# A fused patch, attention and expert kernel: patches resident in the first stage, rows loaded and normed in groups beside the patch products

## What is computed

```python
p = x.reshape(B, C, NH, PH, NW, PW).transpose(0, 2, 4, 3, 5, 1).reshape(B, NH * NW, PH * PW * C)
h = jnp.einsum('bnd,hd->bnh', p, Wp) + b + pos           # 16 images x 64 patches x 256
h = jnp.concatenate([h, txt], axis=1)                    # 16 x 141 x 256
h = h + L0_attn(layernorm(h), Wq, Wkv, Wo)               # 8 heads, l2-normed q and k
h = h + L0_ffn(layernorm(h), ...)                        # 8 experts, top 2
h = h + L1_attn(layernorm(h), ...)
h = h + L1_ffn(layernorm(h), ...)
```

## Time and profile before

| | |
|---|---|
| time, median of 3 runs | 1245.07 us (1244.85 to 1264.2) |
| time of the profiled execution | 1249.64 us |
| its span, first to last instruction | 1247.8 us |
| PE busy | 1066.6 us (85%) |
| DVE busy | 677.3 us (54%) |
| ACT busy | 417.8 us (33%) |
| POOL busy | 367.7 us (29%) |
| mean granted TensorE clock | 0.912 of 2.4 GHz |

### The profile page before, as it was taken

The page is one execution under the profiler, slowest core; times in us unless marked ns, Lnnn a source line. Parts: engine busy times, 40 slices in busy tenths (PEclk is TensorE's granted clock), DMA queues, the critical chain, the costliest instruction groups (busy, mean ns, idle before and its releaser), DMA issues.

```text
span 1247.8 us, 22340 instructions
## 1 busy us (share of the span) xinstructions
PE 1066.6 (85%) x7200; PEld 881.0 (71%) x7200; DVE 677.3 (54%) x1577; ACT 417.8 (33%) x868; POOL 367.7 (29%) x238
## 2 busy tenths in 40 slices
PE   5489979887199999999999994978999999875765
PEld 4368867776178888888888882546878888764634
DVE  0366636666734444444444445975566766545555
ACT  0245555663022222222222212444344444343313
POOL 0000000222461460661506005507444544312104
PEclk8799989998599999999999997998798999786977
DMA  6411144331264414323300003520100011020243
GB/s 240 141 43 47 45 151 138 103 102 35 93 179 153 144 40 144 103 85 140 131 26 31 27 17 110 165 86 26 26 25 25 26 29 28 11 81 14 72 153 123
DMA packets 68699, 104.84 MB, mean 84 GB/s; under 512 B 15141, under 2 KB 53637, under 8 KB 66285
## 3 DMA queue, kind: packets, MB, share of 16 engines
q1 hardware_dynamic: 44941, 52.13, 13.8%
q0 software_dynamic: 5904, 34.61, 7.8%
q10 hardware_dynamic: 17776, 17.04, 4.0%
HBM read 74.60 MB, written 30.41 MB: 84 GB/s over the span
## 4 chain that ended last, share of the span: by engine, by line
PE 66%; DVE 15%; issue 8%; DMA 5%; ACT 4%; POOL 1%; SPq 0%; DVEq 0%; ACTq 0%; POOLq 0%
PE psum L1717 19%; PE psum L1732 10%; PE psum L1573 6%; PE psum L1853 5%; PE psum L1830 4%; PE psum L1725 3%; PE psum L1637 2%; DMA work<-in_patches 2%; PE psum L1843 1%; PE psum L1540 1%; PE psum L1928 1%; PE psum L1877 1%; PE psum L1855 1%; PE psum L1876 1%; PE psum L1976 1%
## 5 line engine op out<-in xcount | busy, mean ns | idle before, releaser
L1221 DVE TENSOR_TENSOR work<-work,psum 128x512 f32<-128x512 f32 x86 | 59.1, 687 | 218.8 <-ACT work L719 218.8
L1717 PE MATMUL psum<-w_high,xT_high 128*128 x344 | 139.5, 406 | 1.1 <-DVE xT_low L1215 1.1
L1717 PE MATMUL psum<-w_low,xT_high 128*128 x344 | 135.2, 393 | 0.0
L1717 PE MATMUL psum<-w_high,xT_low 128*128 x344 | 134.8, 392 | 0.0
L719 ACT ACTIVATE work<-psum 128x512 f32<-128x512 f32 x86 | 51.4, 598 | 207.2 <-PE psum L1717 207.2
L1732 PE MATMUL psum<-w_high,hidT_high 128*128 x344 | 103.6, 301 | 0.6 <-DVE hidT_low L1228 0.6
L1732 PE MATMUL psum<-w_high,hidT_low 128*128 x344 | 96.1, 279 | 0.0
L1732 PE MATMUL psum<-w_low,hidT_high 128*128 x344 | 96.0, 279 | 0.0
L518 POOL TENSOR_TENSOR w_low<-big,w_high 128x6144 fp32r<-128x6144 f32 x7 | 94.2, 13457 | 0.6
L516 POOL CAST w_high<-big 128x6144 fp32r<-128x6144 f32 x7 | 37.3, 5322 | 188.2 <-PE psum L1732 177.3
L1830 PE MATMUL psum<-wexp,work 128*128 128x282 f32 x256 | 83.4, 454 | 7.9 <-POOL wexp L543 7.7
(11 more groups left out here) (287 smaller groups left out, 2341.8 us busy)
## 6 DMA issues: line engine op xcount, KB each, us to landing
big<-in_w_gu POOLq DMA_DIRECT2D x7, 2048.0 KB, 9.0
work<-v_scratch SPq DMA_DIRECT2D x32, 256.0 KB
big<-in_w_down POOLq DMA_DIRECT2D x7, 1024.0 KB, 11.3
work<-slot_in_scratch SPq DMA_DIRECT2D x43, 128.0 KB, 2.0
slot_out_scratch<-work ACTq DMA_DIRECT2D x43, 128.0 KB, 1.7
v_scratch<-work SPq DMA_DIRECT2D x18, 256.0 KB, 2.0
work<-in_rope SPq DMA_DIRECT2D x18, 192.0 KB, 2.4
work<-in_patches SPq DMA_DIRECT2D x8, 384.0 KB, 4.5
```

The source lines that it names most:

```text
L1221: nc.vector.tensor_tensor(hid[:, s, :], sil[:, s, :], psum[:, 2 * s + 1, :], ALU.mult).then_inc(S("hid_ready"), 1)
L1717: m = nc.tensor.matmul(psum[:, 2 * half + a, :], f32r(x_[:, s, k, :]), f32r(w_[:, ds(at + k * 2 * F + a * F + half * 512, 512)]), start=(k ...
```

## The change

All of it lies in the first stage. Nothing of the computation changes.

- The four pairs of patch tiles get four places (`pt_places`), and SP issues all four loads at the start, each of two tiles, with no wait. The patch weight counts on the first pair's semaphore. Of the row vectors only the first comes at the start; the other four come behind the load of group 0.
- PE's tiles go to four PSUM banks instead of two. Its wait for `w0low` moves behind the first transpose.
- `posb` and `h0s` move from `work` to `wexp`.
- The stores of patch tiles go from ACT to SP. SP loads group 0 of `h` after issuing the stores of tile 3, once the stores of tiles 0 to 2 and the text of six images have landed; group 1 after issuing those of tile 6, once the stores of tiles 0 to 5 have landed; group 2 at the end.
- ACT copies the text in two parts: six images, then, behind the weight of the first attention and once the first part has landed, ten. With no stores to issue, it goes on to `w0high` at once.
- DVE keeps tiles 0 to 4, then norms group 0 and the first two tiles, then keeps tiles 5 to 7, then takes `w0low`.

```diff
-        pt = view(work, 0, 2, PK, P)
-        posb = view(work, 1536, D)
-        h0s = view(work, 1792, 2, D)
+        pt_places = (view(work, 0, 2, PK, P), *(view(work, 4912 + 1536 * n, 2, PK, P) for n in range(3)))
+        posb = view(wexp, 6400, D)
+        h0s = view(wexp, 6656, 2, D)
...
 SP
-            sp.dma_start(wtok_sb, w_tok).then_inc(S("tables_ld"), 16)
-            sp.dma_start(posb, pos_table).then_inc(S("tables_ld"), 16)
-            sp.dma_start(rowv[:, :, :], row_vectors).then_inc(S("tables_ld"), 16)
-            with sp.Fori(0, IMAGES // 4) as i:
+            sp.dma_start(wtok_sb, w_tok).then_inc(S("pt_ld0"), 16)
+            for n in range(IMAGES // 4):
+                sp.dma_start(pt_places[n].rearrange("p o k n -> p o (k n)"), patches[2 * n:2 * n + 2, :, :, :].rearrange("o p k n -> o p (k n)")).then_inc(S(f"pt_ld{n}"), 16)
+                if n == 0:
+                    sp.dma_start(posb, pos_table).then_inc(S("tables_ld"), 16)
+                    sp.dma_start(rowv[:, 0, :], row_vectors[:, 0, :]).then_inc(S("tables_ld"), 16)
+
+            def load_group(g, tiles):
                 for s in range(2):
-                    t = 2 * i + s
-                    sp.wait_ge(S("tok_ps"), t + 1)
-                    sp.dma_start(pt[:, s, :, :], patches[ds(t, 1), :, :, :].rearrange("o p k n -> p (o k) n")).then_inc(S(f"pt_ld{s}"), 16)
-
-            sp.wait_ge(S("h0_st"), 32)
-            for s in range(2):
-                sp.wait_ge(S(f"tok_st{s}"), 32 * (IMAGES // 4 + 1))
-            for g in range(GROUPS):
+                    sp.wait_ge(S(f"tok_st{s}"), 32 * ((tiles + 1 - s) // 2))
                 sp.dma_start(h[:, g * GT:(g + 1) * GT, :], h0_d[g * GT * P:(g + 1) * GT * P, :].rearrange("(t p) d -> p t d", p=P)).then_inc(S(f"h_ld{g}"), 16)
+
+            for t in range(IMAGES // 2):
+                sp.wait_ge(S("tok_ready"), t + 1)
+                for r in range(2):
+                    sp.dma_start(h0_img[2 * t + r, 0:PATCHES, :], h0s[64 * r:64 * r + 64, t % 2, :]).then_inc(S(f"tok_st{t % 2}"), 16)
+                if t == 3:
+                    sp.wait_ge(S("h0_st"), 16)
+                    load_group(0, 3)
+                    sp.dma_start(rowv[:, 1:5, :], row_vectors[:, 1:5, :]).then_inc(S("h_ld0"), 16)
+                if t == 6:
+                    sp.wait_ge(S("h0_st"), 48)
+                    load_group(1, 6)
+            load_group(2, IMAGES // 2)
...
 ACT
-            act.wait_ge(S("pt_ld1"), 16)
-            act.dma_start(h0_img[:, PATCHES:SEQ, :], txt).then_inc(S("h0_st"), 16)
+            act.wait_ge(S("pt_ld0"), 32)
+            act.dma_start(h0_img[0:GT, PATCHES:SEQ, :], txt[0:GT, :, :]).then_inc(S("h0_st"), 16)
+            act.dma_start(const[:, :], constants).then_inc(S("w0_ld"), 16)
+            act.dma_start(wqkv_sb, w_qkv0).then_inc(S("w0_ld"), 16)
+            act.wait_ge(S("h0_st"), 16)
+            act.dma_start(h0_img[GT:IMAGES, PATCHES:SEQ, :], txt[GT:IMAGES, :, :]).then_inc(S("h0_st"), 16)
...
-            with act.Fori(0, IMAGES // 4) as i:
-                for s in range(2):
-                    t = 2 * i + s
-                    act.wait_ge(S("tok_ready"), t + 3)
-                    for r in range(2):
-                        act.dma_start(h0_img[ds(2 * t + r, 1), 0:PATCHES, :].rearrange("o n d -> (o n) d"),
-                                      h0s[64 * r:64 * r + 64, s, :]).then_inc(S(f"tok_st{s}"), 16)
...
 DVE
+            def keep_tok(t):
+                dve.wait_ge(S("tok_ps"), t + 1)
+                if t >= 2:
+                    dve.wait_ge(S(f"tok_st{t % 2}"), 32 * (t // 2))
+                nc.vector.tensor_tensor(h0s[:, t % 2, :], psum[:, t % 4, 0:D], posb, ALU.add).then_inc(S("tok_ready"), 1)
+
+            for t in range(5):
+                keep_tok(t)
 
             def norm_group(g):
-                dve.wait_ge(S(f"h_ld{g}"), 16)
+                dve.wait_ge(S(f"h_ld{g}"), 16 if g else 32)
...
             norm_group(0)
             for t in range(2):
                 normed(xn[:, t, :], t).then_inc(S("xn_ready"), 1)
+            for t in range(5, IMAGES // 2):
+                keep_tok(t)
+            dve.wait_ge(S("act_did"), W0_HIGH)
+            step(nc.vector.tensor_tensor(f32r(w0low), wqkv_sb, w0high, ALU.subtract))
+            dve.sem_inc(S("dve_did"), 1)
...
 PE
+            for t in range(IMAGES // 2):
+                if t % 2 == 0:
+                    pe.wait_ge(S(f"pt_ld{t // 2}"), 32 if t == 0 else 16)
+                if t >= 4:
+                    pe.wait_ge(S("tok_ready"), t - 3)
+                for k in range(PK):
+                    m = nc.tensor.matmul(psum[:, t % 4, 0:D], pt_places[t // 2][:, t % 2, k, :], wtok_sb[:, k, :], start=(k == 0), stop=(k == PK - 1))
+                m.then_inc(S("tok_ps"), 1)
 
             pe.wait_ge(S("w0_ld"), 32)
-            pe.wait_ge(S("dve_did"), DID["w0low_ready"])
-            pe.wait_ge(S("tok_ready"), IMAGES // 2 + 2)
+            pe.wait_ge(S("tok_ready"), IMAGES // 2)
...
             def qkv_tile(t, s, first=False, last=False):
                 pe.wait_ge(S("xTl_ready"), t + 3)
+                if first:
+                    pe.wait_ge(S("dve_did"), DID["w0low_ready"])
```

More of the change, by code:

```diff
@@ L371, in _ @@
-            sp.wait_ge(S("h0_st"), 32)
-            for s in range(2):
-                sp.wait_ge(S(f"tok_st{s}"), 32 * (IMAGES // 4 + 1))
-            for g in range(GROUPS):
-                sp.dma_start(h[:, g * GT:(g + 1) * GT, :], h0_d[g * GT * P:(g + 1) * GT * P, :].rearrange("(t p) d -> p t d", p=P)).then_inc(S(f"h_ld{g}"), 16)
+            sp.dma_start(wtok_sb, w_tok).then_inc(S("pt_ld0"), 16)
+            for n in range(IMAGES // 4):
+                sp.dma_start(pt_places[n].rearrange("p o k n -> p o (k n)"), patches[2 * n:2 * n + 2, :, :, :].rearrange("o p k n -> p o (k n)")).then_inc(S(f"pt_ld{n}"), 16)
+                if n == 0:
+                    sp.dma_start(posb, pos_table).then_inc(S("tables_ld"), 16)
+                    sp.dma_start(rowv[:, 0, :], row_vectors[:, 0, :]).then_inc(S("tables_ld"), 16)
@@ L569, in _ @@
         def _(act):
-            act.wait_ge(S("pt_ld1"), 16)
-            act.dma_start(h0_img[:, PATCHES:SEQ, :], txt).then_inc(S("h0_st"), 16)
+            act.wait_ge(S("pt_ld0"), 32)
[4 more added lines that the diff above has]
+            act.dma_start(h0_img[GT:IMAGES, PATCHES:SEQ, :], txt[GT:IMAGES, :, :]).then_inc(S("h0_st"), 16)
             act.wait_ge(S("pool_did"), FILLS)
             act.dma_start(h0_d[IMAGES * SEQ:ROWS, :], zeros[0:ROWS - IMAGES * SEQ, :]).then_inc(S("h0_st"), 16)
-            act.dma_start(const[:, :], constants).then_inc(S("w0_ld"), 16)
-            act.dma_start(wqkv_sb, w_qkv0).then_inc(S("w0_ld"), 16)
-            for s in range(2):
-                act.sem_inc(S(f"tok_st{s}"), 32)
-            with act.Fori(0, IMAGES // 4) as i:
-                for s in range(2):
-                    t = 2 * i + s
-                    act.wait_ge(S("tok_ready"), t + 3)
-                    for r in range(2):
-                        act.dma_start(h0_img[ds(2 * t + r, 1), 0:PATCHES, :].rearrange("o n d -> (o n) d"),
-                                      h0s[64 * r:64 * r + 64, s, :]).then_inc(S(f"tok_st{s}"), 16)
             act.sem_inc(S("xT_ready"), 2)
@@ L960, in normed @@
                 return nc.vector.tensor_scalar(out_, h[:, t, :], mv[:, t, 0:1], rstd[:, ds(t, 1)], ALU.subtract, ALU.mult)
-            dve.wait_ge(S("tables_ld"), 48)
+            dve.wait_ge(S("tables_ld"), 32)
             step(nc.vector.tensor_tensor(posb, posb, rowv[:, 0, :], ALU.add))
[L965 to L977, removed]
+            def keep_tok(t):
[5 more added lines that the diff above has]
+                keep_tok(t)
             def norm_group(g):
-                dve.wait_ge(S(f"h_ld{g}"), 16)
+                dve.wait_ge(S(f"h_ld{g}"), 16 if g else 32)
                 for t in range(g * GT, (g + 1) * GT):
```

## The result

The changed kernel takes 1231.35 us (median of 15 runs, 1226.37 to 1241.78), the kernel before 1251.52 (median of 15, 1238.44 to 1265.26). The ratio is 0.9884, with a 95% interval of 0.9854 to 0.9913: 1.2% faster, between 0.9 and 1.5. The ratio is taken over the fast executions alone, without the slow ones of the kernel before, so it is nearer to 1 than the ratio of the two medians (0.984). The forecast was 17.4 us off 1245.07, 1.4%. The profiled execution took 1236.84 us with a span of 1235.0, 12.8 us under the span of before.

A forecast was written before the change was run, and what follows sets the result against it. PE was taken to bound the whole kernel, a relay of waits the changed stage. The first transposed tile's start moving from 56.38 to 39.0 gives 17.4 us off the median 1245.07: 1227.7 us, range 1219.5 to 1236.5.

The forecast's parts named there:

- The start and the patch products: First stage: PE starts at 7.2 instead of 8.19 and is through with tile 7 at about 29; later patch waits go.
- Group 0: First rows of h through DRAM: load issued at 21.2, landed at 27.4, normed with two tiles by 31.5.
- the far end: Latest bound for landing of tile 2's stores: 8.6 us on the way, 26.3; the near bound was 2.0 us, 19.7.
- a copy that lies on part of the engines: Six-image text copy confined to six DMA engines: lengthens group 0's way by an estimated 3 us at most.
- The store's queue: Patch stores on SP stand behind 1.57 MB of patches, so moving them from ACT does not free them.
- the keeps start at 11.6, 14.1, 16.6, 19.1: DVE's keeps of the first four patch tiles, in us, spaced by 2.49 us per tile after the first.
- The new wait of tile 7: DVE waits about 2.6 us for tile 5's store before keeping tile 7, kept at 35.45; `w0low` follows until 38.9.
- mark: Start of the first `x0T_low` on DVE, the rest of the first transposed tile: 56.38 before, forecast at 39.0.
- Nothing else is paid: Behind the first transposed tile: groups 1 and 2 land in time, PE's clock stays as it was, no further cost.
- the third rival: Contention: stores behind patches land at 26.3, not 21.2, group 0's load takes 8.2, not 6.2; 1234.8 us, chance 0.13.
- within 2%: Whole kernel's time differs by less than 24.9 us, about what a measurement can tell from no change; chance 0.91.

The follow-up runs named there:

- all edits together: Changed kernel with eight stored-tile places, text cut over 16 engines, `w0low` before statistics, four row vectors and PE's last-patch wait later: 1217.13 us, ratio 0.9759 to kernel before.

## Why the prediction was right or wrong, point by point

**The start and the patch products.** PE started at 6.97 (forecast 7.2) and was through with tile 7 at 30.3 (29). All patch waits but the first went. Right, and the run with this part alone shows that it carries the gain. Two things beside it were off. The first tile took 4.5 to 5.6 us from PE's start to its keep, not 4.4, so that without reuse tile 2 was kept at 17.65 or 17.70 and not at 16.6. And "tile 6 needs its pair at 26 and tile 4 at 21.5" are the times at which those tiles are kept; PE needs the pairs one product, 2.5 us, earlier. Nothing came of that, as PE waited for no pair after the first.

**The step that failed.** It is the way of the stores in "Group 0": the load was to be issued at 21.2 and was issued at 27.41, 6.2 us late. Two terms of the sum were wrong.

The larger is the landing, "here the patches and that weight are through at 21, so I take 21.2". With no place reused, the last store of tile 2 was issued 1.0 us later than forecast and landed at 25.53 all the same: 6.9 us on its way, not 3.6. I had given 26.3 as the far end and then taken a value near the other, because I counted bytes over 16 engines. But from 18 to 20 only 10 to 12 of the 16 were at work (DMA share 0.55, and 0.95 with the copies cut). The prediction had weighed a copy that lies on part of the engines, put it at 3 us at most and left it out of the sum; it measured 3.0 us with eight places and 3.9 with two. The store's queue had been weighed too, and a queue of their own took tile 2 from 24.35 to 19.93.

The smaller is "the keeps start at 11.6, 14.1, 16.6, 19.1": I took PE's pace for DVE's. I had seen that tile 7 waits for the store of tile 5, but the same line of code makes tile 2 wait for tile 0, when a store takes longest. Keeps of tiles 2 and 3 came at 24.35 and 24.8.

Run by run the 6.2 us are: 1.8 the reused place (27.41 to 25.61 with eight places), 3.0 the form of the text copies (to 22.60 with both cut), and 1.4 left. Of these 1.4, 1.0 is that tile 2 is kept at 17.65 and not at 16.6, and 0.3 that its last store then takes 3.9 us to land and not 3.6. Taken in the other order the text is 3.9 and the place 0.9.

**Load and norm of group 0.** 5.9 us from issue to landing (forecast 6.2), 4.1 of norms (4.1): right.

**The new wait of tile 7 and `w0low` behind it.** Right in place and size: 2.33 us of DVE's wait, `w0low` at 40.81, mark 4.0 us after the keep of tile 7 as forecast. `w0high` was done at 23.97, off the path. That `w0low` could stand in the 5.4 us for which DVE waits for the load, the prediction did not see; moved there it brought 2.4 us.

**Nothing else is paid.** Right as far as it can be seen. From the mark to the first matmul of the experts it was 289.3 us before and 291.2 after, in one execution each. The first products began at the low level again: the granted clock was 0.50 until 48 and 1.00 from 49, and the first 18 took 5.78 us (6.39 before, 4.20 at the full level throughout).

**The time.** 12.0 us at the mark and 12.8 in the span against 17.4 forecast; over 15 runs the ratio says 14.5 of 1251.5, between 10.9 and 18.3. The forecast's size lies in that interval, and the time lies in its range, but for the reason only in part: in the chain the third rival, contention of the stores (mark at 46.1), was nearer than the forecast (39.0). The 12.0 us of the mark lie in the same interval, so the time does not tell them from 17.4; that it suits the forecast says nothing for the forecast's timetable.

**The chances.** I called 2% about what a measurement can tell and put 0.91 on "within 2%". The change is within 2%, but that premise was wrong: 15 runs tell 1.2% from nothing, with an interval of 0.3% to each side. The text should have said plainly that 1.4% faster was forecast as a real gain. And the third rival's 0.13 was too little: a term that was weighed and called possible, the text on part of the engines, stood on its side.

## What to carry to other kernels

Where a place is reused, write down the wait for each turn of the loop, not for one: the turn that hurts is the one at which the transfer it waits for meets the bulk, and staging places are cheap where SBUF is free. When a store is late with the DMA engines half idle, look for a copy whose outermost dimension is below 16, in flight or queued ahead of what is in flight; here cutting two such copies was worth 3 to 4 us. And before rows are regrouped to overlap, ask what then stands behind the last wait on the in-order engine: here 3.4 us of `w0low` stood at the end of the path, while DVE was idle for 5.4 us a little earlier.

## What was not expected of the hardware

A store of 64 KB takes 1.9 to 2.1 us to land on quiet engines, but 5.5 to 5.7 beside a DRAM to DRAM copy of ten images, with a DMA share of 0.84 and 0.61. The Trainium skill, DMA: Bandwidth & Descriptors, says in its section on queues, rings and completion order that an engine's count for a finished copy lands only after all its earlier writes, across its queues. No run here shows that this is the mechanism. The packets speak for something else beside it: not only the counts but the stores' own packets came late, about half of them after the last text packet had ended, and each text packet is 39 KB long. Nor is the effect peculiar to such a copy. The stores of tile 4, issued right behind the load of group 0 and the row vectors, took 4.9 and 4.7 us in the changed kernel, and 5.0 and 6.4 with the text cut.

Behind the mark, the rest of the span took between 1181.1 and 1196.3 us in single executions of kernels that are the same there. Two executions of the changed kernel alone differ by 8 us: 1235.0 - 44.4 = 1190.6 and 1227.4 - 44.9 = 1182.5. Most of the difference lies in the end of the second attention and right behind it, where the granted clock differs. The windows of the changed kernel, then of its second run:

```profile
950.00:1062.00 112.00, 108.64 (x649) 92.66 (x648) 70.91 (x143) 45.95 (x106) 55.96 (x41) 0.88 0.10 25
1062.00:1090.00 28.00, 19.35 (x80) 16.01 (x80) 7.47 (x19) 5.61 (x15) 0.52 (x1) 0.57 0.23 74
```

```profile
950.00:1058.00 108.00, 105.68 (x644) 89.31 (x643) 72.17 (x146) 46.45 (x107) 55.33 (x41) 0.91 0.10 26
1058.00:1081.00 23.00, 16.00 (x78) 13.44 (x77) 4.52 (x12) 4.59 (x14) 0.00 (x0) 0.65 0.27 87
```

Two stretches of 112 and 28 us took 108 and 23, at 0.91 and 0.65 of the full clock instead of 0.88 and 0.57. A single time of this kernel cannot rank edits worth 4 us; the mark can.

The clock at the first products went with how PE spent the time ahead of them. With all edits together it was idle for 1.65 us, did two transposes and ran the products with a granted clock of 1.00, 2.4 GHz. With places and cut text alone it was idle for 3.26, then 3.32, with two transposes between, and began them at 0.50, 1.2 GHz, as these rows of its timeline show (0.66 us for two transposes, where the other kernel took 0.44):

```profile
33.83 0.66 PE L1560 MATMUL psum<-const,xbuf 128*128 128x128 f32 x2 [3.26 <-issue]
37.81 0.69 PE L1560 MATMUL psum<-const,xbuf 128*128 128x128 f32 x2 [3.32 <-DVE x0T_low L998]
38.15 0.78 PE L1575 MATMUL psum<-w_high,xT_high 128*128 128x512 f32 x1
```
